# One attention table changed: transposes one unit later, and VectorE's two jobs of a step swapped

## The reference

```python
q = rms_norm(x @ wq.T, q_norm_w)          # 32 heads of 64
k = rms_norm(x @ wk.T, k_norm_w)          # 8 key heads, each shared by 4 query heads
v = x @ wv.T
scores = einsum('bhtd,bhsd->bhts', q, k) * 64**-0.5 + bias   # ALiBi; window of 256 keys back, causal
out = einsum('bhts,bhsd->bhtd', softmax(scores), v) @ wo.T
# second layer: (silu(x @ gate.T * gate_s) * (x @ up.T * up_s)) @ down.T * down_s, inner width 1408
```

## Time and profile before

| what | value |
|---|---|
| median of 3 runs | 1289.93 us |
| the profiled execution: time, span | 1292.3 us, 1290.5 us |
| TensorE matmuls busy / weight loads busy | 1202.0 us (93%) / 1009.0 us (78%) |
| VectorE / ScalarE / GpSimd busy | 944.1 us (73%) / 758.4 us (59%) / 389.4 us (30%) |
| mean granted TensorE clock | 0.989 of full speed |

### The profile page before, as it was taken

How to read it: one execution, slowest core, us unless ns; L and a number is a source line. 1 busy time by engine, 2 the same in 40 slices (tenths; PEclk the granted TensorE clock), 3 DMA queues, 4 the chain that set the end, 5 groups by cost and what they waited for, 6 DMA issues and landing times.

```text
span 1290.5 us, 29717 instructions
## 1 busy us (share of the span) xinstructions
PE 1202.0 (93%) x9016; PEld 1009.0 (78%) x9016; DVE 944.1 (73%) x2514; ACT 758.4 (59%) x2013; POOL 389.4 (30%) x459
## 2 busy tenths in 40 slices
PE   5999999997988999999999999999979979999998
PEld 4868778785766778889888898888867758888876
DVE  4597776857989898888888888888854346646364
ACT  3645454554888897877777777777732234232330
POOL 1000000002588775453535444443421100202021
PEclk9999999998999999999999999999989989999999
DMA  4216263455576555544546455554442252111120
GB/s 164 98 74 245 110 232 130 186 199 198 184 248 219 188 175 183 176 157 156 171 157 193 141 186 163 159 168 150 150 151 98 98 181 81 66 33 66 34 66 34
DMA packets 99262, 189.24 MB, mean 147 GB/s; under 512 B 8032, under 2 KB 36832, under 8 KB 99168
## 3 DMA queue, kind: packets, MB, share of 16 engines
q1 hardware_dynamic: 99168, 188.07, 42.7%
HBM read 116.48 MB, written 71.57 MB: 146 GB/s over the span
## 4 chain that ended last, share of the span: by engine, by line
PE 70%; DVE 12%; issue 8%; ACT 4%; POOL 3%; DMA 2%; DVEq 0%; ACTq 0%; POOLq 0%; SPq 0%
PE bank L1247 17%; PE bank L1378 17%; PE bank L1315 12%; PE bank L1278 8%; PE bank L1269 7%; DVE u_sb L1026 3%; ACT p_sb L825 2%; PE bank L1294 2%; PE bank L1304 2%; PE bank L1296 2%; PE bank L1295 2%; DVE pT_lo L1033 2%; DVE inv_rms L980 2%; POOL bias L607 1%; POOL qk L642 1%
## 5 line engine op out<-in xcount | busy, mean ns | idle before, releaser
L825 ACT ACTIVATE p_sb<-u_sb,low 128x384 f32<-128x384 f32 (+2 forms) x512 | 273.7, 535 | 74.5 <-DVE low L1026 47.5
L1026 DVE CUSTOM_DVE_ANT_0 u_sb<-bank,bias 128x384 f32<-128x384 f32 (+2 forms) x512 | 231.7, 453 | 37.2 <-PE bank L1269 17.8
L1033 DVE TENSOR_TENSOR pT_lo<-bank,pT_hi 128x384 f16<-128x384 f32 (+2 forms) x512 | 232.4, 454 | 28.9 <-ACT pT_hi L833 18.7
L1269 PE MATMUL bank<-k_st,q_st 128*128 128x384 f32 (+2 forms) x1024 | 247.2, 323 | 4.4 <-DVE v_out L1000 2.9
L1278 PE MATMUL bank<-ident,p_sb 128*128 128x128 f32 x1152 | 220.9, 282 | 29.1 <-DVE pT_lo L1033 19.2
L833 ACT ACTIVATE pT_hi<-bank 128x384 f16<-128x384 f32 (+2 forms) x512 | 204.0, 398 | 45.4 <-PE bank L1278 43.6
L1269 PEld LDWEIGHTS bank<-k_st,q_st 128*128 128x128 f32 x1024 | 175.4, 191 | 27.7 <-DVE v_out L1000 3.3
L1278 PEld LDWEIGHTS bank<-ident,p_sb 128*128 128x128 f32 x1152 | 137.1, 141 | 75.9 <-ACT p_sb L825 49.9
L580 POOL TENSOR_TENSOR rstd<-var_eps,minus_half 128x1 f32<-128x1 f32 (+1 forms) x31 | 23.3, 752 | 492.1 <-DVE var_eps L921 492.1
L617 POOL TENSOR_TENSOR o_mid<-o_raw,inv_sum 128x256 f32<-128x256 f32 x128 | 84.1, 657 | 241.1 <-DVE o_raw L1047 239.5
L1294 PE MATMUL bank<-v_st,pT_hi 128*128 128x64 f16 x1152 | 154.7, 193 | 0.5 <-DVE pT_lo L1033 0.5
(11 more groups left out here) (115 smaller groups left out, 2424.1 us busy)
## 6 DMA issues: line engine op xcount, KB each, us to landing
q_scr<-qk SPq DMA_DIRECT2D x64, 512.0 KB, 2.7
q_st<-q_scr SPq DMA_DIRECT2D x32, 1024.0 KB, 7.8
k_st<-k_scr SPq DMA_DIRECT2D x64, 256.0 KB, 3.0
o_scr<-o_out SPq DMA_DIRECT2D x128, 128.0 KB, 2.6
o_in<-o_scr SPq DMA_DIRECT2D x16, 1024.0 KB, 5.3
k_scr<-qk SPq DMA_DIRECT2D x16, 512.0 KB, 2.8
z_in<-z_scr SPq DMA_DIRECT2D x8, 1024.0 KB, 6.0
x_in<-x SPq DMA_DIRECT2D x4, 1024.0 KB, 8.3
```

Source lines behind the costliest of these rows:

```text
L825: nc.scalar.activation(p_sb[:, u % RING, 0:w], u_sb[:, u % RING, 0:w], ACT.Exp, scale=-1.0, bias=low[:, u % RING:u % RING + 1], accum_out= ...
L1026: nc.vector.tensor_tensor_reduce(out=u_sb[:, u % RING, 0:w], in0=bank[u % 2][:, 0:w], in1=bias[:, 2 * u // UNITS, u % REP, at:at + w], sca ...
L1033: nc.vector.tensor_tensor(pT_lo[:, u % RING, 0:w], bank[2 + u % 2][:, 0:w], pT_hi[:, u % RING, 0:w], ALU.subtract).then_inc(pT_ready, 1)
L1269: mm = nc.tensor.matmul(bank[u % 2][:, 0:w], q_st[:, s, r, P * i:P * i + P], k_st[:, s, part, P * key:P * key + w], start=(part == 0), sto ...
```

## The change

One line changes. The transposes and the rounding, which share the stage "transpose", run three units behind the scores instead of two. The stage "split" is written after "scores" and "transpose" instead of first; its lag stays 3.

```diff
-LAGS = {"split": 3, "scores": 0, "transpose": 2, "exps": 0, "invert_sums": 1, "weigh": 4, "take": 5}
+LAGS = {"scores": 0, "transpose": 3, "split": 3, "exps": 0, "invert_sums": 1, "weigh": 4, "take": 5}
```

## The result

The changed kernel takes 1352.27 us (median of 4 runs, 1351.18 to 1353.17) against 1290.44 for the kernel before in the same comparison. The ratio is 1.0475, 95% interval 1.0460 to 1.0491: slower by 61.8 us. Forecast were +39 us, 1329 us, and a range of 1296 to 1352, so the measured time stands at its upper end. The profiled execution has a span of 1351.1 us.

What follows compares the result with a forecast made beforehand. Without projection it took a VectorE and ScalarE loop of 1.15 us a step as the bound, with projection TensorE in most steps. +10 (first groups) and +29 (projection groups) gave +39 us, 1329 us; range 1296 to 1352.

Steps and rivals of the forecast that it cites:

- Bias ahead of split: Attention, VectorE's order: the same four operations still loop over two steps, 2.3 us, 1.15 a step; gain 0.
- Transposes to values in one turn: TensorE's queue in attention: rounding and split must fit in one turn instead of two; half without projection 17.0 against 15.57 us.
- the loop of 2.42 us: Three-tile units without projection: values, scores, transposes, rounding, split back to values over two steps, 1.21 a step against 1.15.
- Groups with projection, +2.7 each: Groups 5 to 15: head of group and VectorE side work lose 2.7 us a group, +29 us over 11 groups.
- the steps 0 to 8: Head of a group with projection: VectorE, already saturated, idles in the new order; scores(9) start at 10.5 instead of 9.46, +1.05.
- the backlog of step 12: Groups with projection: copy and oT split fall together, 1.0 us, ahead of the next bias and split; values wait, +0.5.
- steps 16 to 23: Groups with projection, forecast as steps 18 to 22: 2.8 us of side work puts VectorE behind, values wait, +0.7.
- the backlog of step 24: Groups with projection: copy and oT split fall together again, with two tiles, +0.45.
- Groups 0 to 4, +10: Ten halves without projection: +1.4 us each, +14, part of it covered, taken as +10; ends +5 and +16.
- cover: Groups 0 to 2: some copies wait for GpSimd's scaling, so later copies wait less; +14 taken as +10.
- Rival (c): Values wait for everything on VectorE, side work shows in every group: 1366 us, chance 0.07; a falling clock would add.

Runs made afterwards that it cites:

- swap alone: Kernel before with only the order changed: VectorE takes bias ahead of split, transposes and rounding stay two units behind; 1350.82 us, ratio 1.0468.
- the memset: VectorE's part of the 14 late normalizations replaced by an 8-column memset: 1333.53 us in the changed kernel, 1286.32 in the kernel before.
- values at 5: Changed kernel with values five units behind instead of four and the copy six: 1309.11 us, ratio 1.0142.

## Why the prediction was right, and where it was wrong

The sign and the cause are as forecast; the size is 1.6 times the forecast. The time is inside the range by luck: the first five groups lose 25 us, more than the +16 that the range allowed them, and the room that it left for the groups with projection (up to +41) made up for it.

**Bias ahead of split gives nothing.** Right that it gains nothing: with the bias first and the distance to the values restored, halves take 16.0 to 16.5 us, not less than 15.57. But the swap alone costs 59 us by a loop that the forecast did not look at, through the bank that the transposes wait for. In the changed kernel the lag of 3 opens that loop (no wait at L1278 is left), and the one through the values closes.

**Transposes to values in one turn.** Right: the wait stands at L1294 and names the split, and with the distance restored 43 of 62 us go. A half group was put at 17.0 and measures 17.06 (17.02 in the mean of four). Its last five steps take 1.13, 1.24, 1.13, 1.34 and 1.24 us, 1.22 in the mean, where the loop of 2.42 us gives 1.21.

**Groups with projection, +2.7 each.** Measured 3.05 in a middle group, and each term stands where it was put. Against the kernel before, the steps 0 to 8 lose 1.41 us (1.05 forecast; the mis-sized term: VectorE's idle time grew by 1.03, from 9.46 - 9.10 to 10.87 - 9.48, and its busy time by 0.38, which the forecast had at nothing), the backlog of step 12 shows at step 14 with 0.46 (0.5), steps 16 to 23 lose 0.78 (0.7), the backlog of step 24 shows at step 26 with 0.41 (0.45).

**Groups 0 to 4, +10.** Wrong: measured +25. The undisturbed halves pay 1.45 (1.4 forecast). What failed is in groups 0 to 2, where the forecast counted GpSimd's scaling as cover and gave the late normalizations beside it no price. The cover may well be there: with the late normalizations reading nothing in both orders, these groups lose 5.5 us, less than six halves at 1.45, and all five lose 11.4. Single executions don't show such a difference surely. The price is what was left out, 14.6 us: 61.8 less the 47.2 that stay when the late normalizations read nothing. The prediction treated VectorE and GpSimd as joined by semaphores alone. A normalization with two SBUF inputs also waits for the end of an instruction of GpSimd that reads SBUF and has started before it. In the old order VectorE's comes first (357.74 against 358.10) and GpSimd pays; in the new order it comes second and pays itself, with TensorE behind it. The Trainium skill has this rule ("SBUF — State Buffer", Who interferes with whom): a VectorE instruction with two SBUF inputs contends with a GpSimd instruction that reads SBUF, and whoever comes second is fully blocked. The trace agrees on both sides: 2.76 us for 512 columns and 2.37 for 8 behind GpSimd, and 3.20 instead of 2.75 for GpSimd behind VectorE.

**The clock.** Rival (c) named it as an addition and doubted it. It came, in groups 0 to 2: 0.82 instead of 0.97 over 316 to 436 us. It fell to 0.50, the lower of the two levels (1.2 of 2.4 GHz), in the stretches behind those waits (370 to 375 us in the changed kernel), where steps 9 and 10 take 1.55 us each; in group 3, at full clock, they take 0.98 and 1.20. It was at that level also from 318.5 to 335.5 us, at the start of attention, against 316.1 to 323.0 in the kernel before; two normalizations of 1.41 and 1.49 us, held behind GpSimd's low halves, fall in that time. In all it spent 42 of these 120 us there, against 7. An estimate from these rows: 3.10 us for 2.18 is 0.3 us lost for each of the 35 more, so up to about 10 of the 19.5 us can be the clock's. How the 14.6 us divide between the blocked instructions and the clock stays open: the memset took both away (clock 0.94 in that stretch in either order).

**What stays open besides.** With values at 5 the first three groups still lose 10.9 us, which moving one normalization does not change. Between 316 and 436 us TensorE's weight loads for the scores wait 16.1 us for the bias step there, against 2.0 in the kernel before, and the clock is 0.87. No run takes this apart.

## What to carry to other kernels

In a software pipeline over in-order queues, go round every loop: add up the operations of all engines between a unit and the unit some steps on that waits for it, bank reuse included, and divide by the steps. A lag raised on one stage takes a step from the next distance, and an order swapped within a step takes the bias's time from it; neither shows in busy shares. Where two engines overlap, ask for each pair of side jobs whether both read SBUF, and which of them starts first in the new order: a job of 0.75 us can stand for 2.8.

## What the runs showed of the hardware

- A VectorE instruction with two SBUF inputs (L959) that starts during GpSimd's bias product is held until that ends, whatever its own size: 8 columns 2.37 us, 512 columns 2.76, behind products of 2.75. With no SBUF input it takes 0.07, and with one in SBUF and one in PSUM a bias step takes its usual 0.55. Where VectorE starts first, GpSimd's product takes 3.20 us.
- Handovers differ by what waits. From the end of a split to the values that wait for it 0.06 us (changed kernel), to transposes that wait for it 0.15 (swap alone). From the start of three-tile scores to the bias step that waits for them 0.73 us in groups with projection (kernel before), 0.81 in groups without (swap alone).
